# Feed-forward stages: the mean of squares taken by two float32r matmuls, one step later

## The chip, the cores and the metric

The kernel runs on one core of a Trainium2 chip. The core has five engines with queues of their own that meet only at semaphores: TensorE (PE, matmuls into PSUM; its weight loads are listed as PEld), VectorE (DVE), ScalarE (ACT), GpSimd (POOL) and SyncE (SP, which issues the DMAs). The metric is the device time of one execution in microseconds.

## The reference

A batch of 4 sequences of 1024 tokens with 128 channels goes through four blocks, each with a layer norm ahead of it and a residual around it: a first attention, a feed-forward stage, a causal attention, and the same feed-forward stage again. The change lies in the feed-forward stage, which runs twice. Each of its two layers is

```python
h = shift_token(x)                       # half of the channels comes from the token before
q, k, v = split(h @ wqkv, 3)             # 8 heads of 64
q, k = rotary_xpos(l2norm(q) * qs, l2norm(k) * ksc)
x = x + local_attention(q, k, v) @ wo    # windows of 64, the window before and its own
h = shift_token(x)
h = (h - h.mean(-1)) / sqrt(h.var(-1) + 1e-05) * lg + lb
a, g = split(h @ w1 + b1, 2)
x = x + (a * gelu(g)) @ w2 + b2
```

What changes is how `h.var` is computed: the mean over the channels of the squares of the centred `h`.

## The kernel before, in words

`ffn_stage` keeps channels on the partitions. Its work is cut into 64 tiles of 128 tokens (2 layers, 8 places, 4 sequences); four tiles of one place are a group `g`, and 512 columns of the second half of the layer (shift, norm, the two products `W1` and `W2`) are done for a whole group at a time. A loop over steps `i` is written out once for each engine, and at each step an engine does its parts of several tiles: the projection of tile `i+2` (`project_qk`, `project_v`), the transposes (`turn`) of tile `i+1`, the scores of tile `i`, the transposes of the probabilities (`turn_probs`) of tile `i-1` and the product with the values (`attend`) of tile `i-2`. Nothing but this order and the semaphores sets when something runs.

The parts of a group are hung on certain steps by `mlp_at`: "wo" at the second of four steps, "centre" and "mean" at the third, "w2" at the third or fourth, "gate01" at the fourth. At the third step PE multiplies `H2` by the centring matrix into the bank `m_ps[:, 0, :]` (L507), ACT squares that bank into `SQ2` (L657), and PE, as the last thing of the step, multiplies `SQ2` by the matrix `mean` (every entry 1/128) into `m_ps[:, 1, :]` (L561), in float32. At the next step ACT takes the logarithm and the exponential of that bank (L630, L632), which gives the reciprocal of the root, and DVE multiplies the centred bank by it into `HN` (L754).

The queues around this place, in order, are these. PE, third step: scores (L412, L421), centre (L507), `turn_probs` (L433), `turn` (L398), mean (L561); fourth step: `project_qk` (L379, which waits for DVE's copy `PT`, L786), `project_v` (L388, which waits for ACT's copy `QT`, L668), `attend` (L449), scores, `W2` (L500). ACT, third step: squares for the query norm (L638, which waits for DVE's rotary products L747), two copies (L649, L604), the square `SQ2`, eight exponentials of the scores (L594), the copy `QT`; fourth step: logarithm and exponential of the variance, then L638 again. POOL, every step: probabilities times reciprocal (L841), rotary sum (L847), a power (L853), which waits for DVE's clamped sums (L799).

Of the kernel before, what the change touches and what calls it, by code (L numbers as in the profile page):

```python
# [6 lines left out]
P = 128  # L7
NB, T = 4, 1024
NT = T // P
PAD = 4  # L10
EPS = 1e-5
F32 = mybir.dt.float32
# [138 lines left out]
def ffn_stage(nc, d, keep, stage):  # L151
# [5 lines left out]
    with nc.cleanup_on_exit(), ExitStack() as ctx:  # L157
# [33 lines left out]
        G = sb("G", [HC, NHC, NB * P])  # L191
        AG = sb("AG", [HC, NHC, NB * P])
        w0_ps, w1_ps, s_ps, m_ps = (ps(n, [P, 2, 512]) for n in ("w0", "w1", "s", "m"))
        nsq, nrs = [SQ2, H2], [RS, HN]

        s_set, s_qkv, s_qkv1, s_mlp_w, s_wo, s_w2, s_bias, s_folded, s_w1, s_rope, s_rope1, s_scaled, s_zero = (
# [24 lines left out]
        def real(x):  # L221
            return 0 <= x < TILES
# [40 lines left out]
        def norm_at(i):  # L263
            return i + EARLY if EARLY <= i + EARLY < NT and i >= 0 else None
# [68 lines left out]
        def _(pe):  # L333
            xt = X[:, :].rearrange("p (b t) -> p b t", b=NB)

            def norm_centre(t):
                if t >= EARLY:
                    pe.wait_ge(n_out, t)
                    pe.wait_ge(s_folded, 1)
                elif t >= 2:  # L340
                    pe.wait_ge(n_out, t - 1)
                pe.matmul(centre_bank(t), keep["centre"][:, :], xt[:, :, t * P:(t + 1) * P], start=True, stop=True)\
                  .then_inc(n_centred, 1)
# [109 lines left out]
            def hidden(g, half, j):  # L453
                pe.matmul(mlp_bank(g, half, j), W1[:, g // NT, half, j, :], HN[:, :], start=True, stop=True)\  # L454
                  .then_inc(gate_mm if half else value_mm, 1)

            norm_centre(0)
            norm_centre(1)
            norm_mean(0)
# [3 lines left out]
            for i in STEPS:  # L463
                g = mlp_at(i, "value1")
                if g is not None and g < LAST:
                    pe.wait_ge(gelu, 3 * g + 3)
                    hidden(g, 0, 1)
                if real(i + 2):
                    project_qk(i + 2)
                if norm_at(i) is not None:  # L470
                    norm_centre(norm_at(i))
                if real(i - 2) and values_first(i):
                    attend(i - 2)
                g = mlp_at(i, "gate2")
                if g is not None and g < LAST:
                    pe.wait_ge(gelu, 3 * g + 1)
                    hidden(g, 1, 2)
                if real(i + 2):
                    project_v(i + 2)
                g = mlp_at(i, "value0")  # L480
                if g is not None and g < LAST:
                    pe.wait_ge(hid, 3 * g + 1)
                    hidden(g, 0, 0)
                if real(i - 2) and not values_first(i):
                    attend(i - 2)
                if real(i):
                    score(i)
                if i == -1:
                    fold_bias()
                if norm_at(i) is not None:  # L490
                    norm_mean(norm_at(i))
                g = mlp_at(i, "w2")
                if g is not None:
                    pe.wait_ge(hid, 3 * g + 3)
                    if g + 1 < LAST:
                        pe.wait_ge(lnvar, g + 2)
                    if g == 0:
                        pe.wait_ge(s_w2, 16)
                    for j in range(NHC):
                        last = pe.matmul(m_ps[:, 1, :], W2[:, g // NT, j, :], AG[:, j, :], start=(j == 0),  # L500
                                         stop=(j == NHC - 1))
                    last.then_inc(w2_mm, 1)
                g = mlp_at(i, "centre")
                if g is not None:
                    pe.wait_ge(u, g + 1)
                    pe.wait_ge(s_h2[g % 2], 32 * (g // 2 + 1))
                    pe.matmul(m_ps[:, 0, :], keep["centre"][:, :], H2[:, :], start=True, stop=True).then_inc(centre_mm, 1)  # L507
                g = mlp_at(i, "value2")
                if g is not None and g < LAST:
                    pe.wait_ge(gelu, 3 * g + 2)  # L510
                    hidden(g, 0, 2)
                g = mlp_at(i, "gate01")
                if g is not None:
                    pe.wait_ge(hn, g + 1)
                    if g % NT == 0:
                        pe.wait_ge(s_w1, g // NT + 1)
                    if g < LAST:
                        hidden(g, 1, 0)
                if real(i - 1):
                    turn_probs(i - 1)  # L520
                if g is not None:
                    if g == LAST:
                        pe.wait_ge(pt, TILES)
                        pe.wait_ge(ot, TILES)
                        pe.wait_ge(kt, TILES)
                        pe.wait_ge(qt, TILES)
                        pe.wait_ge(probs, 2 * TILES)
                    elif g >= 1:
                        pe.wait_ge(ynext, g)
                    if g == LAST:  # L530
                        hidden(g, 1, 0)
                    hidden(g, 1, 1)
                    if g == LAST:
                        hidden(g, 1, 2)
                        hidden(g, 0, 2)
                        hidden(g, 0, 1)
                        hidden(g, 0, 0)
                if real(i + 1):
                    turn(i + 1)
                g = mlp_at(i, "wo")  # L540
                if g is not None:
                    pe.wait_ge(ot, NB * (g + 1))
                    if g >= 1:
                        pe.wait_ge(hid, 3 * g - 1)
                    else:
                        pe.wait_ge(n_out, NT)
                        pe.wait_ge(s_wo, 16)
                    for p in range(NPAIR):
                        last = pe.matmul(m_ps[:, 0, :], Wo[:, g // NT, p, :], OT[:, g % 2, p, :, :], start=(p == 0),
                                         stop=(p == NPAIR - 1))  # L550
                    last.then_inc(wo_mm, 1)
                g = mlp_at(i, "mean")
                if g is not None:
                    pe.wait_ge(sq2, g + 1)
                    if g >= 1:
                        pe.wait_ge(hid, 3 * g)
                    else:
                        pe.wait_ge(n_ln, NT)
                    if g == LAST:
                        pe.wait_ge(ynext, g)  # L560
                    pe.matmul(m_ps[:, 1, :], keep["mean"][:, :], SQ2[:, :], start=True, stop=True).then_inc(mean_mm, 1)  # L561

        @block.scalar
        def _(act):
# [48 lines left out]
            for i in STEPS:  # L613
# [39 lines left out]
                if g is not None:  # L653
                    act.wait_ge(centre_mm, g + 1)
                    if g >= 1:
                        act.wait_ge(mean_mm, g)
                    act.activation(SQ2[:, :], m_ps[:, 0, :], ACT.Square).then_inc(sq2, 1)  # L657
                if norm_at(i) is not None:
                    norm_square(norm_at(i))
                if real(i):  # L660
# [154 lines left out]
        def _(pool):  # L815
            pool.memset(mhalf[:, :], -0.5).then_inc(s_zero, 1)
            pool.memset(KT[:, :, :, :, :, :], 0.0).then_inc(s_zero, 1)
            pool.memset(Voff[:, :, :], 0.0).then_inc(s_zero, 1)

            def scale_rope(l, tiles):  # L820
                n = tiles.stop - tiles.start
# [13 lines left out]
            for i in STEPS:  # L835
                if real(i - 1):
                    x = i - 1
                    pool.wait_ge(rden, x + 1)
                    probs_x = PB[:, x % 2, :, :, :].rearrange("p e q k -> p (e q) k")
                    by = RDEN[:, x % 2, :, :].rearrange("p e q -> p (e q)").unsqueeze(2).broadcast_to([P, NH, P])  # L840
                    pool.tensor_tensor(probs_x, probs_x, by, ALU.mult).then_inc(normed, 1)  # L841
                if real(i + 2):
                    x = i + 2
                    pool.wait_ge(roped, x + 1)
                    if x >= 2:
                        pool.wait_ge(turned, 2 * x - 2)
                    pool.tensor_tensor(QK[:, x % 2, :, :, :].rearrange("p c q k -> p (c q k)"),  # L847
                                       T1[:, :, :, :].rearrange("p c h k -> p (c h k)"),
                                       T2[:, :, :, :].rearrange("p c h k -> p (c h k)"), ALU.add).then_inc(rope_sum, 1)
                    pool.wait_ge(clamped, x + 1)  # L850
                    if x >= 2:
                        pool.wait_ge(scaled, x - 1)
                    pool.tensor_tensor(RN[:, x % 2, :], SS[:, x % 2, :], mhalf[:, :], ALU.pow).then_inc(rnorm, 1)  # L853
                if i == 2:
                    pool.wait_ge(s_rope1, 16)
                    scale_rope(1, slice(0, NT))
# [1469 lines left out]
```

## Time and profile before

| | |
|---|---|
| median of 3 runs | 2151.45 us (2147.72 to 2151.94) |
| the profiled execution's own time | 2163.37 us |
| its span, from first to last instruction | 2161.6 us |
| mean granted TensorE clock | 0.967 |
| busy share of the span: PE, DVE, ACT, POOL | 92%, 83%, 63%, 57% |
| PE busy in the group from 430.30 to 471.20 us | 40.85 of 40.90 us |

A row of the timeline has the start in us from the span's start, the duration in us, the engine, the line, the operation, what it writes and reads, the shape, how many instructions were merged, and in brackets the idle time of the engine before it with what ended it. A float32 matmul stands in two instructions. PE's instructions are pipelined: each is listed until its result has drained, so the next one starts before it ends, and the distance of two starts is what one costs on PE.

### The profile page before, as it was taken

How to read it: one execution, taken by the hardware profiler on the slowest of the kernel's cores; microseconds unless marked ns; L12 is line 12 of the kernel's file. 1: busy time of each engine (PE TensorE's matmuls, PEld its weight loads, DVE VectorE, ACT ScalarE, POOL GpSimd, SP SyncE). 2: the span in 40 equal slices, each digit the busy share in tenths (PEclk: the TensorE clock that was granted, in tenths of full speed). 3: DMA queues.
4: the chain of work that ended last, by engine and by line, in shares of the span. 5: the costliest groups of instructions: out<-in, count | busy, mean ns of one | idle time of the engine just before them, and what ended most of it. 6: DMA issues, size and time to landing. Idle time of an engine off the chain costs nothing. (4 is left out here: it accounts for less than half of the span.)

```text
span 2161.6 us, 45550 instructions
## 1 busy us (share of the span) xinstructions
PE 1997.2 (92%) x16998; PEld 1096.8 (51%) x16998; DVE 1793.7 (83%) x2383; ACT 1366.5 (63%) x3435; POOL 1234.0 (57%) x599
## 2 busy tenths in 40 slices
PE   5686899999999999799999999967999999999997
PEld 2233555555555555345544444424555565555553
DVE  6986799999999996447888888537999999999993
ACT  8454566666666666325777777746667667666663
POOL 0116778778877875424222222247887877777770
PEclk9799999999999999969999999989999999999999
DMA  2003111211111110231322222022111111211111
GB/s 64 0 1 113 49 36 36 50 36 36 45 40 36 42 34 21 69 122 29 113 55 50 56 48 54 19 81 66 45 41 36 41 41 34 45 41 35 38 34 44
DMA packets 85473, 101.38 MB, mean 47 GB/s; under 512 B 13504, under 2 KB 60552, under 8 KB 83208
## 3 DMA queue, kind: packets, MB, share of 16 engines
q1 hardware_dynamic: 82824, 96.77, 17.8%
q8 instruction: 138, 2.26, 0.4%
q10 hardware_dynamic: 2432, 1.70, 0.3%
q14 instruction: 79, 0.65, 0.1%
HBM read 33.94 MB, written 10.49 MB: 21 GB/s over the span
## 5 line engine op out<-in xcount | busy, mean ns | idle before, releaser
L853 POOL TENSOR_TENSOR ffn_RN<-ffn_SS,ffn_mhalf 128x16 f32<-128x16 f32 x128 | 372.5, 2910 | 267.8 <-DVE ffn_SS L799 267.4
L2000 DVE TENSOR_REDUCE attn_b_NX<-attn_b_s 128x1 f32<-128x512 f32 (+3 forms) x608 | 365.1, 656 | 80.8 <-PE attn_b_s L1701 78.8
L847 POOL TENSOR_TENSOR ffn_QK<-ffn_T 128x1024 f32<-128x1024 f32 x128 | 420.4, 3284 | 20.1 <-DVE ffn_T L747 19.9
L594 ACT ACTIVATE ffn_PB<-ffn_s,ffn_NM 128x128 f32<-128x128 f32 x1024 | 360.3, 386 | 101.4 <-DVE ffn_NM L769 101.1
L1918 ACT ACTIVATE attn_b_PT<-attn_b_s 128x1024 f32<-128x1024 f32 (+1 forms) x320 | 284.0, 939 | 123.8 <-PE attn_b_s L1735 123.4
L638 ACT ACTIVATE ffn_SQ<-ffn_w 128x1024 f32<-128x1024 f32 x128 | 131.1, 1024 | 308.1 <-DVE ffn_T L747 307.7
L841 POOL TENSOR_TENSOR ffn_PB<-ffn_PB,ffn_RDEN 128x1024 f32<-128x1024 f32 x128 | 243.6, 1903 | 26.7 <-DVE ffn_RDEN L732 26.7
L379 PE MATMUL ffn_w<-ffn_Wqkv,ffn_H 128*128 128x512 f32 x512 | 245.4, 602 | 11.7 <-ACT ffn_SQ L638 4.7
L763 DVE TENSOR_TENSOR ffn_QK<-ffn_QK,ffn_RN 128x1024 f32<-128x1024 f32 x128 | 249.7, 1951 | 1.4 <-POOL ffn_RN L853 0.3
L594 ACT ACTIVATION_READ_ACCUMULATOR ffn_PB<-ffn_s,ffn_NM 128x1 f32 x1024 | 231.3, 226 | 0.0
L1701 PE MATMUL attn_b_s<-attn_b_KS,attn_b_QS 62*128 62x512 f32 (+3 forms) x768 | 228.2, 411 | 0.2
L786 DVE COPY ffn_PT<-ffn_w 128x1024 f32<-128x1024 f32 x128 | 156.2, 1220 | 74.3 <-PE ffn_w L433 74.3
L454 PE MATMUL ffn_m<-ffn_HN,ffn_W 128*114 128x512 f32 x360 | 189.3, 608 | 2.0 <-ACT ffn_G L622 2.0
L1735 PE MATMUL attn_b_s<-attn_b_QS,attn_b_KS 64*128 64x512 f32 (+3 forms) x768 | 171.9, 388 | 4.7 <-DMA attn_b_QS<-attn_b_MT 3.0
L744 DVE TENSOR_TENSOR ffn_T<-ffn_w,ffn_rope 128x1024 f32<-128x1024 f32 x128 | 154.3, 1205 | 19.2 <-PE ffn_w L379 19.1
L1754 PE MATMUL attn_b_o<-attn_b_PT,attn_b_VQ 128*32 128x512 f32 (+3 forms) x1536 | 165.3, 503 | 0.2
L747 DVE TENSOR_TENSOR ffn_T<-ffn_w,ffn_rope 128x512 f32<-128x512 f32 x256 | 163.6, 681 | 0.0
L449 PEld LDWEIGHTS ffn_w<-ffn_PT,ffn_Voff 128*64 128x64 f32 x2048 | 106.8, 137 | 108.4 <-issue 101.0
L769 DVE TENSOR_REDUCE ffn_NM<-ffn_s 128x8 f32<-128x1024 f32 x128 | 155.3, 1213 | 1.4 <-PE ffn_s L421 1.4
L379 PEld LDWEIGHTS ffn_w<-ffn_Wqkv,ffn_H 128*128 128x128 f32 x512 | 95.0, 193 | 121.1 <-issue 82.2
L796 DVE TENSOR_REDUCE ffn_SS<-ffn_SQ 128x16 f32<-128x1024 f32 x128 | 154.6, 1208 | 2.2 <-ACT ffn_SQ L638 2.2
L433 PEld LDWEIGHTS ffn_w<-ident,ffn_PB 128*128 128x128 f32 x1024 | 117.1, 143 | 76.4 <-issue 58.4
(250 smaller groups left out, 3791.4 us busy)
## 6 DMA issues: line engine op xcount, KB each, us to landing
ffn_Voff<-ffn_Vcur SPq DMA_DIRECT2D x248, 128.0 KB, 2.3
ffn_H<-ffn_Y SPq DMA_DIRECT2D x64, 128.0 KB, 2.5
ffn_H<-ffn_U SPq DMA_DIRECT2D x64, 128.0 KB, 2.5
attn_b_QS<-attn_b_qk_parts SPq DMA_DIRECT2D x64, 128.0 KB
attn_b_KS<-attn_b_qk_parts SPq DMA_DIRECT2D x64, 128.0 KB
attn_b_qk_parts<-attn_b_RP SPq DMA_DIRECT2D x6, 1024.0 KB, 7.5
ffn_rope<-in_ffn_rope_dram SPq DMA_DIRECT2D x4, 1024.0 KB, 7.8
attn_b_rope<-attn_b_OS SPq DMA_DIRECT2D x252, 16.0 KB
```

The costliest lines, as they stand in the source:

```text
L379: last = pe.matmul(w0_ps[:, c, :], H1[:, g % 2, b, :], Wqkv[:, l, c, :], start=True, stop=True)
L454: pe.matmul(mlp_bank(g, half, j), W1[:, g // NT, half, j, :], HN[:, :], start=True, stop=True)\
L594: last = act.activation(PB[:, x % 2, e, p, :], s_ps[:, e, p * P:(p + 1) * P], ACT.Exp, bias=NM[:, x % 2, e, p:p + 1], accum_out=DEN[:, x % ...
L763: dve.tensor_tensor(qk, qk, RN[:, x % 2, :].unsqueeze(2).broadcast_to([P, 2 * NH, DH]), ALU.mult)\
L841: pool.tensor_tensor(probs_x, probs_x, by, ALU.mult).then_inc(normed, 1)
L847: pool.tensor_tensor(QK[:, x % 2, :, :, :].rearrange("p c q k -> p (c q k)"), T1[:, :, :, :].rearrange("p c h k -> p (c h k)"), T2[:, :, : ...
L853: pool.tensor_tensor(RN[:, x % 2, :], SS[:, x % 2, :], mhalf[:, :], ALU.pow).then_inc(rnorm, 1)
L1701: last = pe.matmul(bank[:, q * width:(q + 1) * width], QS[rows, m % RING, pr, i * P:(i + 1) * P], KS[rows, m % RING, pr, c * 512:c * 512 + ...
L1735: last = pe.matmul(bank[par][:, q * w:(q + 1) * w], KS[rows, n % RING, first + q, j * P:(j + 1) * P], QS[rows, n % RING, first + q, lo:hi] ...
L1754: last = pe.matmul(o_ps[VCOLS * g:VCOLS * (g + 1), lo - half * 512:512], VQ[:, n % 2, g, j, :], PT[:, (n * NPIECE + s) % PRING, g, 0:hi - ...
L1918: act.activation(out, bank, ACT.Exp).then_inc(probs, 1)
L2000: dve.tensor_reduce(at, bank, AX_X, ALU.max, negate=True).then_inc(s1_read, 1)
```

## The change

The float32 matmul of `SQ2` by `mean` at the end of the third step goes. [...] POOL makes `meanr` once at the start of a stage.

```diff
+        SQH, SQL = (sb(name, [P, NB * P], F32R) for name in ("SQH", "SQL"))
+        meanr = sb("meanr", [P, P], F32R)
...
+            def mean_square(g):
+                if g == 0:
+                    pe.wait_ge(s_meanr, 1)
+                    pe.wait_ge(n_ln, NT)
+                else:
+                    pe.wait_ge(hid, 3 * g)
+                if g == LAST:
+                    pe.wait_ge(ynext, g)
+                pe.wait_ge(sq_hi, g + 1)
+                pe.matmul(m_ps[:, 1, :], meanr[:, :], SQH[:, :], start=True, stop=False)
+                pe.wait_ge(sq_lo, g + 1)
+                pe.matmul(m_ps[:, 1, :], meanr[:, :], SQL[:, :], start=False, stop=True).then_inc(mean_mm, 1)
...
                 if real(i + 2):
                     project_qk(i + 2)
+                g = mlp_at(i - 1, "mean")
+                if g is not None:
+                    mean_square(g)
...
-                g = mlp_at(i, "mean")
-                if g is not None:
-                    pe.wait_ge(sq2, g + 1)
-                    if g >= 1:
-                        pe.wait_ge(hid, 3 * g)
-                    else:
-                        pe.wait_ge(n_ln, NT)
-                    if g == LAST:
-                        pe.wait_ge(ynext, g)
-                    pe.matmul(m_ps[:, 1, :], keep["mean"][:, :], SQ2[:, :], start=True, stop=True).then_inc(mean_mm, 1)
...
                     act.activation(SQ2[:, :], m_ps[:, 0, :], ACT.Square).then_inc(sq2, 1)
+                    act.wait_ge(sq2, g + 1)
+                    act.activation(SQH[:, :], SQ2[:, :], ACT.Copy).then_inc(sq_hi, 1)
...
+            pool.tensor_copy(meanr[:, :], keep["mean"][:, :]).then_inc(s_meanr, 1)
...
+                g = mlp_at(i, "centre")
+                if g is not None:
+                    pool.wait_ge(sq_hi, g + 1)
+                    pool.tensor_tensor(SQL[:, :], SQ2[:, :], SQH[:, :].bitcast(F32), ALU.subtract).then_inc(sq_lo, 1)
+                if real(i + 2):
+                    x = i + 2
                     pool.wait_ge(clamped, x + 1)
```

The first place is PE's queue at the seam of the third and fourth step of a group, before the change; `ffn_SQ` stands for `SQ2`, `ffn_H` in the centre row for `H2`.

```order
L421 MATMUL ffn_s<-ffn_KT,ffn_QT 64x128 x16
L507 MATMUL ffn_m<-ffn_H,centre 128x512
L433 MATMUL ffn_w<-ident,ffn_PB 128x128 x8
L398 MATMUL ffn_w<-ident,ffn_QK 128x128 x8
L561 MATMUL ffn_m<-ffn_SQ,mean 128x512
L379 MATMUL ffn_w<-ffn_Wqkv,ffn_H 128x512 x2
L388 MATMUL ffn_w<-ffn_Wqkv,ffn_H 128x512
```

And the same place after the change, where the lines after the new code have moved by a few.

```order
L424 MATMUL ffn_s<-ffn_KT,ffn_QT 64x128 x16
L526 MATMUL ffn_m<-ffn_H,centre 128x512
L436 MATMUL ffn_w<-ident,ffn_PB 128x128 x8
L401 MATMUL ffn_w<-ident,ffn_QK 128x128 x8
L382 MATMUL ffn_w<-ffn_Wqkv,ffn_H 128x512 x2
L469 MATMUL ffn_m<-ffn_SQH,ffn_meanr 128x512
L471 MATMUL ffn_m<-ffn_SQL,ffn_meanr 128x512
L391 MATMUL ffn_w<-ffn_Wqkv,ffn_H 128x512
```

The mean has left the place between the transposes (L398, now L401) and `project_qk`, and its two successors stand between `project_qk` and `project_v`.

The second place is ACT's queue at the same step, after the change; before it, the row of `SQH` is absent and the others stand in the same order.

```order
L647 ACTIVATE ffn_SQ<-ffn_w 128x1024
L658 ACTIVATE ffn_Vcur<-ffn_w 128x512
L613 ACTIVATE ffn_OT<-ffn_w 128x4x128
L666 ACTIVATE ffn_SQ<-ffn_m 128x512
L668 ACTIVATE ffn_SQH<-ffn_SQ 128x512
L603 ACTIVATE ffn_PB,ffn_DEN<-ffn_s,ffn_NM 128x128 x8
L679 ACTIVATE ffn_QT<-ffn_w 128x512
L639 ACTIVATE ffn_RS<-ffn_m,eps 128x512
```

The new copy stands ahead of the eight exponentials and of `QT` (L679, before L668).

The third is POOL's queue at that step and the next, after the change.

```order
L853 TENSOR_TENSOR ffn_PB<-ffn_PB,ffn_RDEN 128x1024
L859 TENSOR_TENSOR ffn_QK<-ffn_T 128x1024
L865 TENSOR_TENSOR ffn_SQL<-ffn_SQ,ffn_SQH 128x512
L871 TENSOR_TENSOR ffn_RN<-ffn_SS,ffn_mhalf 128x16
L853 TENSOR_TENSOR ffn_PB<-ffn_PB,ffn_RDEN 128x1024
```

The subtraction stands between the rotary sum and the power. The queues of DVE and SP hold the same instructions in the same order as before.

## Rows read from the trace of the kernel before

**Rows 1.** The page, engines: busy us, share of the span, instructions.

```profile
PE 1997.2 (92%) x16998; PEld 1096.8 (51%) x16998; DVE 1793.7 (83%) x2383; ACT 1366.5 (63%) x3435; POOL 1234.0 (57%) x599
```

**Rows 2.** Busy time of each engine in one group of four steps.

```profile
430.30:471.20 40.90, 40.85 (x392) 24.13 (x391) 38.36 (x48) 27.62 (x89) 32.23 (x13) 1.00 0.17 40
```

**Rows 3.** Timeline of PE and its weight loads, seam of third and fourth step.

```profile
471.79 1.04 PE L398 MATMUL ffn_w<-ident,ffn_QK 128*128 128x128 f32 x8
...
472.67 1.02 PE L561 MATMUL ffn_m<-ffn_SQ,mean 128*128 128x512 f32 x2
...
473.27 0.45 PEld L379 LDWEIGHTS ffn_w<-ffn_Wqkv,ffn_H 128*128 128x128 f32 x2 [0.41 <-DVE ffn_PT L786]
...
473.53 1.88 PE L379 MATMUL ffn_w<-ffn_Wqkv,ffn_H 128*128 128x512 f32 x4
...
475.18 0.30 PEld L388 LDWEIGHTS ffn_w<-ffn_Wqkv,ffn_H 128*128 128x128 f32 x2 [0.60 <-ACT ffn_QT L668]
475.24 1.06 PE L388 MATMUL ffn_w<-ffn_Wqkv,ffn_H 128*128 128x512 f32 x2
...
478.53 2.84 PE L500 MATMUL ffn_m<-ffn_AG,ffn_W 114*128 114x512 f32 x6
```

**Rows 4.** Timeline of ACT, the same third step and the start of the fourth.

```profile
469.36 1.03 ACT L638 ACTIVATE ffn_SQ<-ffn_w 128x1024 f32<-128x1024 f32 x1 [4.24 <-DVE ffn_T L747]
...
471.24 0.62 ACT L657 ACTIVATE ffn_SQ<-ffn_m 128x512 f32<-128x512 f32 x1
...
471.71 0.40 ACT L594 ACTIVATE ffn_PB<-ffn_s,ffn_NM 128x128 f32<-128x128 f32 x1
...
474.45 0.68 ACT L668 ACTIVATE ffn_QT<-ffn_w 128x512 f32<-128x512 f32 x1
...
474.93 0.78 ACT L630 ACTIVATE ffn_RS<-ffn_m,eps 128x512 f32<-128x512 f32 x1
...
475.73 0.63 ACT L632 ACTIVATE ffn_RS<-ffn_RS 128x512 f32<-128x512 f32 x1
```

**Rows 5.** Timeline of DVE and POOL, from the third step to the fourth.

```profile
465.19 0.69 DVE L712 TENSOR_TENSOR ffn_U<-ffn_m,ffn_Y 128x512 f32<-128x512 f32 x1 [0.43 <-PE ffn_m L549]
...
469.25 1.22 DVE L763 TENSOR_TENSOR ffn_QK<-ffn_QK,ffn_RN 128x1024 f32<-128x1024 f32 x1
...
469.41 3.27 POOL L847 TENSOR_TENSOR ffn_QK<-ffn_T 128x1024 f32<-128x1024 f32 x1 [0.39 <-DVE ffn_T L747]
...
471.99 1.23 DVE L786 COPY ffn_PT<-ffn_w 128x1024 f32<-128x1024 f32 x1 [0.40 <-PE ffn_w L433]
...
473.13 1.21 DVE L796 TENSOR_REDUCE ffn_SS<-ffn_SQ 128x16 f32<-128x1024 f32 x1
...
474.63 2.91 POOL L853 TENSOR_TENSOR ffn_RN<-ffn_SS,ffn_mhalf 128x16 f32<-128x16 f32 x1 [1.95 <-DVE ffn_SS L799]
...
475.07 0.19 DVE L732 RECIPROCAL ffn_RDEN<-ffn_DEN 128x8 f32<-128x8 f32 x1
475.44 1.23 DVE L744 TENSOR_TENSOR ffn_T<-ffn_w,ffn_rope 128x1024 f32<-128x1024 f32 x1 [0.19 <-PE ffn_w L379]
...
477.51 1.90 POOL L841 TENSOR_TENSOR ffn_PB<-ffn_PB,ffn_RDEN 128x1024 f32<-128x1024 f32 x1
...
478.38 2.11 DVE L763 TENSOR_TENSOR ffn_QK<-ffn_QK,ffn_RN 128x1024 f32<-128x1024 f32 x1
```

**Rows 6.** Timeline of PE in the causal attention, whose operands are float32r tiles.

```profile
1205.28 0.40 PE L1701 MATMUL attn_b_s<-attn_b_KS,attn_b_QS 62*128 62x512 f32 x2
1205.50 0.41 PE L1735 MATMUL attn_b_s<-attn_b_QS,attn_b_KS 64*128 64x512 f32 x2
```

**Rows 7.** Groups by line: a POOL subtraction into float32r; busy us, mean ns.

```profile
L2082 POOL TENSOR_TENSOR attn_b_RP<-attn_b_TA,attn_b_RP 128x1024 fp32r<-128x1024 f32 x4 | 9.4, 2363 | 6.4 <-ACT attn_b_RP L1843 6.4
```

**Rows 8.** Timeline at the end of the first feed-forward stage, its last group.

```profile
869.88 0.60 ACT L657 ACTIVATE ffn_SQ<-ffn_m 128x512 f32<-128x512 f32 x1 [9.04 <-PE ffn_m L507]
870.53 1.12 PE L561 MATMUL ffn_m<-ffn_SQ,mean 128*128 128x512 f32 x2 [0.69 <-ACT ffn_SQ L657]
871.70 0.69 ACT L630 ACTIVATE ffn_RS<-ffn_m,eps 128x512 f32<-128x512 f32 x1 [1.22 <-PE ffn_m L561]
```

More of the change, by code:

```diff
@@ L193, in ffn_stage @@
         w0_ps, w1_ps, s_ps, m_ps = (ps(n, [P, 2, 512]) for n in ("w0", "w1", "s", "m"))
+        SQH, SQL = (sb(name, [P, NB * P], F32R) for name in ("SQH", "SQL"))
+        meanr = sb("meanr", [P, P], F32R)
+        s_meanr, sq_hi, sq_lo = sem("meanr"), sem("sq_hi"), sem("sq_lo")
         nsq, nrs = [SQ2, H2], [RS, HN]
```

## The prediction

> **What bounds the kernel now.** I read the page first, then the busy time of one group of four steps, then the timeline of the seam where the change lies. The page gives PE 92% of the span [rows 1], and within a group PE is listed busy for 40.85 of 40.90 us at full granted clock (1.00), while DVE has 38.36, POOL 32.23 and ACT 27.62 [rows 2]. So in the two feed-forward stages the order of PE's queue sets the pace, and another engine matters where it makes PE wait. That listing counts a matmul until it has drained, so short holes don't show in it; they show as starts further apart than the stream needs. A float32 instruction with 512 columns takes 0.43 us of stream: the four of `project_qk` start at 473.53 and what follows starts at 475.24, 1.71 us later [rows 3].
>
> At the seam two other engines are only just in time. `project_qk` needs DVE's copy `PT`, which runs from 471.99 and ends at 473.22 [rows 5]; its weights load at 473.27 with that copy named as the releaser, during the mean matmul, which streams from 472.67 to 473.53 [rows 3]. So the old mean filled a time in which PE had nothing else that it could do. Then `project_v` needs ACT's copy `QT`, which ends at 475.13 (474.45 + 0.68) [rows 4]; its weights load at 475.18, released by `QT`, and PE is free at 475.24 [rows 3]. Slack: none. I read these times for all groups: 28 of the 32 (14 in each stage) show this pattern; the last two groups of a stage differ, since no projection follows them.
>
> ACT at this place is one chain without a hole: it waits for DVE until 469.36, and from there to the end of `QT` each instruction starts before the one ahead has ended [rows 4]. The root of that chain is PE's product with `Wo`, for which DVE's `U` waits at 465.19 [rows 5]. So PE (`Wo`), DVE, ACT and PE (`project_v`) form a loop that goes round once in a group, and whatever lengthens ACT's part delays `project_v` by the same amount.
>
> **The change part by part.**
>
> *The mean leaves its old place.* That takes 0.86 us of stream (472.67 to 473.53) from PE. `project_qk` can't use it: its weights still load at 473.27, since `PT` is no earlier. Weights loaded while PE stands idle put off the first columns by about 0.1 us (475.18, then 475.71 for the second instruction of `project_v`, which is 0.10 more than one stream; the 475.71 is 475.24 + 1.06 less the 0.59 that a single instruction is listed, which is 1.88 less three times 0.43). So `project_qk` starts at 473.38 instead of 473.53 and ends at 475.09 instead of 475.24: 0.15 us of the 0.86 is gained, the rest becomes a hole.
>
> *The two new matmuls.* No row shows a float32r matmul with 128 rows. The nearest rows are those of the causal attention, whose tiles are float32r with 64 rows: one instruction for each product instead of two, and the next pair starts 0.22 us after the one before [rows 6]. Two of them cost 0.43 us, to 475.52. The lower bound is nothing (a price below that has no reason), the upper the float32 price of 0.85 each. I take 0.43, since the rows are of the same type and column count. At this price PE is ready for `project_v` at 475.52, which is 0.28 later than before, though half of the stream time was saved. In float32 it would be 475.09 + 1.71 = 476.80.
>
> *The copy `SQH` on ACT.* It stands between the square and the exponentials, and waits for the end of the square. The pair of logarithm and exponential shows the price of such a wait on the instruction just before: 474.93 + 0.78 = 475.71, and the next starts at 475.73 and takes 0.63 with SBUF on both sides [rows 4]. Now the square starts at 471.24 and the first exponential at 471.71, 0.15 before the square ends. With the copy: square to 471.86, copy from 471.88 to 472.51, first exponential 0.15 before that at 472.36. All that follows on ACT in this step is 0.65 us later; `QT` ends at 475.78. The bounds are 0.48 (no wait between the two, the mere distance of square and exponential) and 0.9; nothing lets it be hidden, since ACT has no idle time from 469.36 on.
>
> *What `QT` makes late.* The weights of `project_v` load at 475.83 instead of 475.18. PE, ready at 475.52, waits, and the rest of the group moves by 0.65 us: behind `project_v` in the queue stand the products with the values, the scores and `W2`, which is what starts at 478.53 [rows 3], and they all stream on. The next place where PE waits for others comes a step later and hangs on events after this one, so nothing is caught up there.
>
> *The exponentials also feed DVE.* The reciprocal at 475.07 needs their sums, which then are complete at 475.30; the rotary product after it, which now starts at 475.44 on PE's word, starts at about 475.47 [rows 5]. Nothing is lost there. The logarithm needs the mean matmul (475.52 and its drain, about 475.75) and follows `QT` at 475.8 anyway; DVE uses its result only after its three rotary products, for which it needs until about 478 (475.47 + 1.23 and as much again).
>
> *The subtraction on POOL.* The same subtraction of the same type stands in the causal attention, 2363 ns for 1024 columns [rows 7], so 1.18 us for 512; POOL's rotary sum of 1024 takes 3.27 beside DVE's work [rows 5], which would be 1.64. POOL is free at 472.68 (469.41 + 3.27) and `SQH` ready at 472.51, so `SQL` runs from 472.72 to between 473.9 and 474.4. The power at 474.63 waits for DVE until then [rows 5]: the subtraction lies in POOL's idle 1.95 us, and PE asks for it at 475.3. Cost: nothing. If it took 2.4 us, the power would slip by half a microsecond, and the work on POOL that follows it has more room than that before PE wants it.
>
> A row bears on whether POOL here slows DVE: the product of `QK` and `RN` takes 1.22 us when it starts before POOL's sum, and 2.11 when it starts at 478.38 inside POOL's product of 477.51 to 479.41 [rows 5]. The Trainium skill, "SBUF — State Buffer", section "Who interferes with whom", says that a VectorE instruction meets GpSimd only if both of its inputs lie in SBUF or it is in a two-port mode, and that a reduction never does on this chip. By that rule the reduction at 473.13 stays at 1.21 us under the subtraction and the third rival below falls; without it, it would be a likelier one. The rule agrees with the two rows, but no row has a POOL instruction beside this reduction.
>
> *The ends of the stages.* In the last group nothing else runs, so the chain is serial. Before: square to 870.48, mean from 870.53, logarithm at 871.70 [rows 8]. After: copy to 871.13, subtraction from 871.21 to 872.39, second matmul 0.11 + 0.21 + 0.21 until the logarithm (871.70 - 870.53 less the stream of 0.85 and 0.11 for the weights leaves 0.21), so 872.97: 1.27 us later. The group before it gets ACT's 0.65. That is 1.92 a stage, 3.8 for both. `meanr` is made while POOL waits for a table's DMA: nothing.
>
> *The sum.* 28 x 0.65 = 18.2, plus 3.8: 22.0 us. The profiled execution took 2163.4 us, so it would take 2185.4; the median of the timed runs is 11.9 us lower, and with the same difference the median comes to 2173.4, **2173 us** in round numbers.
>
> **The rivals.**
>
> *ACT isn't the one that decides (2162 us).* The timed runs are 11.9 us faster than the profiled one, up to 0.37 us a group; if that lies in ACT's chain, `QT` comes early enough, and only the hole before `project_qk` is left: 0.24 to 0.28 us a group, 28 x 0.24 + 3.8 = 10.5. For it speaks that difference; against it the unbroken chain of rows 4.
>
> *PE alone sets the pace, and the kernel gets faster (2143 us).* If `PT` and `QT` both came 0.6 us earlier against PE than the profile shows, `project_qk` would follow the transposes at once and PE would save 0.43 us a group: -12 + 3.8 = -8. It decides from the point at which the weights of `project_qk` load before 472.67. Against it: the load at 473.27 names `PT`, whose own wait names PE's transposes, so this chain is tied to PE and can't shift against it by much.
>
> *POOL holds DVE (2182 us).* If DVE's reduction at 473.13 were held until the subtraction ends, up to 1.2 us, DVE's chain of that step would come 1.2 later, the gelu of the fourth step after it, and the group would lose about 0.95 instead of 0.65: 28 x 0.95 + 3.8 = 30.4.
>
> *float32r is no cheaper (2199 us).* With 0.85 for each matmul `project_v` starts at 476.80, 1.52 later: 42.6, and with the ends some 48.
>
> **How the numbers follow.** Chances: the forecast 0.66, ACT not deciding 0.18, POOL holding DVE 0.08, float32r no cheaper 0.03, PE alone 0.05. What a measurement can tell from no change is about 0.2%, 4 us. Faster takes 0.04 of the last, and same takes the remaining 0.01 and 0.04 of a case in which timed runs have nearly the slack to hide it; slower is 0.91. The range, 2159 to 2184, holds the forecast with its bounds for the copy (28 x 0.48 and 28 x 0.9, with the 3.8, give 2169 and 2180), ACT not deciding and POOL holding DVE, with about 2 us either way for the clock at the ends of the stages, where PE idles and is granted half in some stretches.
>
> **What would show it.** In the profile after: the weights of `project_v` at the fourth step load about 0.65 us later after the square than the present 3.94, released by `QT`; the weights of `project_qk` still name `PT`; a hole before each. The two new matmuls are one instruction each, 0.2 us apart. POOL's power still waits for DVE's sums. A group of 40.9 us takes 41.5. If groups are shorter than now, or the load of `project_v` is released by PE's own queue, the loop through ACT was not what binds, and the forecast is wrong.

## The result, and the profile after

The changed kernel takes 2173.35 us (median of four runs, 2166.44 to 2178.53), the kernel before 2149.59 beside it (2146.86 to 2151.94): a ratio of 1.0108, 95% interval 1.0071 to 1.0146, so 15 to 31 us more. The forecast was 2173 in a range of 2159 to 2184. The profiled execution took 2178.2 us with a span of 2176.5.

First the page's row of engines after (columns as in [rows 1]), then the busy time from one square to the next (columns as in [rows 2]), in a group of the kernel before and in one of the changed kernel.

```profile
PE 1995.9 (92%) x16998; PEld 1097.7 (50%) x16998; DVE 1796.7 (83%) x2383; ACT 1393.3 (64%) x3467; POOL 1275.1 (59%) x633
```

```profile
430.30:471.24 40.94, 40.90 (x392) 24.17 (x391) 38.40 (x48) 27.66 (x90) 32.27 (x13) 1.00 0.17 40
```

```profile
516.56:558.17 41.61, 40.93 (x392) 24.11 (x390) 38.27 (x48) 28.44 (x90) 33.49 (x14) 1.00 0.17 39
```

PE is listed busy for 1.3 us less in the whole, and the clock of the group is the full one, yet the group takes 41.61 us where it took 40.94 from square to square. The row of engines can't show the loss: in the stretch between the two stages alone PE is listed busy for 5.5 us less (604.03 and 598.55, in the last section), at another share of half clock. The lengthening is the same through a stage: the second to the ninth distance of two squares are near 40.94 before and near 41.61 after, the next four near 41.54 and 42.22. The first distance of each stage stays what it was (40.52 and 40.39 before, 40.41 and 40.41 after), and the last two vary between executions by up to a microsecond.

What happens stands in the timeline of the seam of third and fourth step (start us, duration us, engine, line, operation; in brackets the idle time before and its releaser). `ffn_SQH` is ACT's float32r copy of the squares, `ffn_SQL` what POOL's subtraction of that copy leaves, and `ffn_meanr` the float32r copy of the matrix `mean`:

```profile
558.17 0.62 ACT L666 ACTIVATE ffn_SQ<-ffn_m 128x512 f32<-128x512 f32 x1
...
558.82 0.63 ACT L668 ACTIVATE ffn_SQH<-ffn_SQ 128x512 fp32r<-128x512 f32 x1
558.93 1.23 DVE L797 COPY ffn_PT<-ffn_w 128x1024 f32<-128x1024 f32 x1 [0.40 <-PE ffn_w L436]
559.36 0.35 ACT L603 ACTIVATE ffn_PB<-ffn_s,ffn_NM 128x128 f32<-128x128 f32 x1
...
559.58 1.27 POOL L865 TENSOR_TENSOR ffn_SQL<-ffn_SQ,ffn_SQH 128x512 fp32r<-128x512 f32 x1
...
560.07 1.21 DVE L807 TENSOR_REDUCE ffn_SS<-ffn_SQ 128x16 f32<-128x1024 f32 x1
...
560.21 0.30 PEld L382 LDWEIGHTS ffn_w<-ffn_Wqkv,ffn_H 128*128 128x128 f32 x2 [0.68 <-DVE ffn_PT L797]
560.21 1.98 PE L382 MATMUL ffn_w<-ffn_Wqkv,ffn_H 128*128 128x512 f32 x4 [0.45 <-DVE ffn_PT L797]
...
561.57 2.91 POOL L871 TENSOR_TENSOR ffn_RN<-ffn_SS,ffn_mhalf 128x16 f32<-128x16 f32 x1 [0.71 <-DVE ffn_SS L810]
...
561.63 0.80 PE L469 MATMUL ffn_m<-ffn_SQH,ffn_meanr 128*128 128x512 f32 x1
...
562.10 0.64 ACT L679 ACTIVATE ffn_QT<-ffn_w 128x512 f32<-128x512 f32 x1
562.26 0.40 PE L471 MATMUL ffn_m<-ffn_SQL,ffn_meanr 128*128 128x512 f32 x1
562.28 0.20 DVE L743 RECIPROCAL ffn_RDEN<-ffn_DEN 128x8 f32<-128x8 f32 x1 [0.20 <-ACT ffn_PB L603]
...
562.79 0.30 PEld L391 LDWEIGHTS ffn_w<-ffn_Wqkv,ffn_H 128*128 128x128 f32 x2 [0.57 <-ACT ffn_QT L679]
562.79 1.13 PE L391 MATMUL ffn_w<-ffn_Wqkv,ffn_H 128*128 128x512 f32 x2
```

Count everything from the start of the square. `project_qk` loads its weights at 2.04 as before (2.03, [rows 3]), still released by `PT`, and PE idles 0.45 us ahead of it. PE is ready for `project_v` at 4.32: the columns of `project_qk` begin 0.10 after the load and stream for 1.71, to 562.02, and two instructions of 0.23 follow, the second at 562.26. (The first is listed from 561.63, while `project_qk` still streams, so here the distance of the two listed starts isn't the price.) But `QT` ends at 4.57 (before 3.89), and the weights of `project_v` load at 4.62 (before 3.94), 0.30 us after PE is ready, with `QT` as the releaser. In all 28 groups that have this seam the load stands 4.60 to 4.62 after the square, before 3.92 to 3.94. The first exponential stands at 1.19 after the square (before 0.47, [rows 4]).

The rows that answer to [rows 6, 7] are groups by line (busy us, mean ns of one):

```profile
L865 POOL TENSOR_TENSOR ffn_SQL<-ffn_SQ,ffn_SQH 128x512 fp32r<-128x512 f32 x32 | 40.6, 1269 | 35.1 <-ACT ffn_SQH L668 35.0
...
L471 PE MATMUL ffn_m<-ffn_SQL,ffn_meanr 128*128 128x512 f32 x32 | 13.0, 406 | 2.3 <-POOL ffn_SQL L865 2.3
```

One instruction a product, 32 for 32 groups, and 0.23 us of stream each (from the end of `project_qk` at 562.02 to 562.26; in the split on POOL below from 476.43 to 476.66): float32r has the price that the attention's tiles showed. The end of the first stage answers to [rows 8]; the logarithm starts 3.19 us after the square, where it started 1.82 after it:

```profile
881.08 0.60 ACT L666 ACTIVATE ffn_SQ<-ffn_m 128x512 f32<-128x512 f32 x1 [9.03 <-PE ffn_m L526]
881.71 0.63 ACT L668 ACTIVATE ffn_SQH<-ffn_SQ 128x512 fp32r<-128x512 f32 x1
882.41 1.27 POOL L865 TENSOR_TENSOR ffn_SQL<-ffn_SQ,ffn_SQH 128x512 fp32r<-128x512 f32 x1 [14.77 <-ACT ffn_SQH L668]
...
883.74 0.49 PE L471 MATMUL ffn_m<-ffn_SQL,ffn_meanr 128*128 128x512 f32 x1 [0.79 <-POOL ffn_SQL L865]
884.27 0.69 ACT L639 ACTIVATE ffn_RS<-ffn_m,eps 128x512 f32<-128x512 f32 x1 [1.94 <-PE ffn_m L471]
```

### The profile page after: what moved, and what is told of

Read it like the earlier page. It is cut to its first block and busy times, and to the rows that moved or that the text cites. A ratio compares the mean times of both kernels' runs of the same rounds, so it can differ in the third digit from the quotient of the medians.

```text
span 2176.5 us, 45616 instructions
## 1 busy us (share of the span) xinstructions
PE 1995.9 (92%) x16998; PEld 1097.7 (50%) x16998; DVE 1796.7 (83%) x2383; ACT 1393.3 (64%) x3467; POOL 1275.1 (59%) x633
## 5 line engine op out<-in xcount | busy, mean ns | idle before, releaser
L871 POOL TENSOR_TENSOR ffn_RN<-ffn_SS,ffn_mhalf 128x16 f32<-128x16 f32 x128 | 372.8, 2913 | 250.3 <-DVE ffn_SS L810 249.9
L603 ACT ACTIVATION_READ_ACCUMULATOR ffn_PB<-ffn_s,ffn_NM 128x1 f32 x1024 | 222.1, 217 | 0.0
```

What stands on the lines that cost most here:

```text
L603: last = act.activation(PB[:, x % 2, e, p, :], s_ps[:, e, p * P:(p + 1) * P], ACT.Exp, bias=NM[:, x % 2, e, p:p + 1], accum_out=DEN[:, x % ...
```

## The experiments

The theory: `project_v` starts at the later of two arrivals, PE's own queue and `QT` through ACT, and the group follows that start one for one. The rivals were that PE's work alone counts, that POOL holds DVE, and that the new place, not the copy, costs the time. All were timed in five rounds against the kernel before. "Group" is the distance of neighbouring squares in a typical group of that run's profile (before 40.94).

| kernel | us | ratio, 95% interval | group |
|---|---|---|---|
| copy alone | 2164.68 | 1.0085, 1.0056 to 1.0113 | 41.61 |
| new place alone | 2167.19 | 1.0091, 1.0059 to 1.0124 | 41.61 |
| split on POOL | 2163.12 | 1.0055, 1.0029 to 1.0081 | 41.21 |
| one float32r matmul, old place | 2150.28 | 1.0002, 0.9977 to 1.0028 | 40.95 |
| after, values ahead of `project_v` | 2166.74 | 1.0077, 1.0049 to 1.0104 | 41.41 |
| before, values ahead of `project_v` | 2162.23 | 1.0042, 1.0017 to 1.0067 | 41.16 |
| split at the old place | 2170.54 | 1.0105, 1.0072 to 1.0138 | 41.68 |

The kernel before took 2145.60 beside the first four and 2150.81 beside the last three. The ratio isn't the quotient of the two medians: single executions of the kernel before lie between 2137.73 and 2159.85 us, and ratio and quotient differ by up to 0.3%.

**The copy alone.** The kernel before, with ACT's copy, which nobody reads.

```
...
                     act.activation(SQ2[:, :], m_ps[:, 0, :], ACT.Square).then_inc(sq2, 1)
+                    act.wait_ge(sq2, g + 1)
+                    act.activation(SQH[:, :], SQ2[:, :], ACT.Copy).then_inc(sq_hi, 1)
```

> The kernel before with one thing added: ScalarE copies the squares into a float32r tile right after squaring; nobody reads the copy, and the float32 mean stays at its old place. Theory (the loop through ScalarE: its exponentials and QT come later, and project_v waits for QT): project_v's weights load 0.65 us later after the square (3.94 becomes about 4.6), a group takes 40.94 + 0.66 = 41.6 us, in all 28 x 0.66 and 0.65 at the end of each stage = about +20 us. Rival (PE's hole before project_qk is what costs): the hole is still filled by the mean, so no change.

Timeline of its seam, whose square starts at 473.62:

```profile
475.90 1.88 PE L381 MATMUL ffn_w<-ffn_Wqkv,ffn_H 128*128 128x512 f32 x4
...
477.55 0.63 ACT L672 ACTIVATE ffn_QT<-ffn_w 128x512 f32<-128x512 f32 x1
...
478.23 0.30 PEld L390 LDWEIGHTS ffn_w<-ffn_Wqkv,ffn_H 128*128 128x128 f32 x2 [1.28 <-ACT ffn_QT L672]
```

PE's side is untouched (`project_qk` at 2.28 after the square, before 2.29), and `project_v` still loads at 4.61. The copy on ACT is enough by itself for the whole loss of a group.

**The new place alone.** The kernel before, with its float32 mean moved behind `project_qk`.

```
...
                     project_qk(i + 2)
+                g = mlp_at(i - 1, "mean")
+                if g is not None:
...
+                    pe.matmul(m_ps[:, 1, :], keep["mean"][:, :], SQ2[:, :], start=True, stop=True).then_inc(mean_mm, 1)
...
```

> The kernel before with one thing moved: the float32 mean stands between project_qk and project_v of the next step; no split, no copy, no subtraction. Theory (the old mean filled a hole that PT leaves, so 0.71 of its 0.86 us become visible): project_qk starts 0.15 earlier, project_v can start at 475.09 + 0.86 = 475.95 in the clock of the first trace instead of 475.28, a group takes 0.66 longer, about +18 us in all. Rival (only ScalarE's copy counts, moving work within PE's queue costs nothing): no change.

Its seam, square at 475.24:

```profile
477.27 1.98 PE L379 MATMUL ffn_w<-ffn_Wqkv,ffn_H 128*128 128x512 f32 x4 [0.44 <-DVE ffn_PT L786]
...
478.45 0.68 ACT L668 ACTIVATE ffn_QT<-ffn_w 128x512 f32<-128x512 f32 x1
...
479.09 1.02 PE L479 MATMUL ffn_m<-ffn_SQ,mean 128*128 128x512 f32 x2
479.52 0.19 PEld L388 LDWEIGHTS ffn_w<-ffn_Wqkv,ffn_H 128*128 128x128 f32 x1 [0.24 <-issue]
479.95 1.02 PE L388 MATMUL ffn_w<-ffn_Wqkv,ffn_H 128*128 128x512 f32 x2
```

Here the releaser is another: the weights of `project_v` are loaded ahead ("issue", no `QT`), for `QT` ended at 479.13, and PE's queue is what comes last, at 4.71. So the move of a float32 mean costs as much as the copy. In the changed kernel, where the shorter matmuls make PE ready at 4.32, the two delays don't add: the group is 41.61 there too.

**The split on POOL.** The changed kernel, with `SQH` copied by POOL.

```
-                    act.wait_ge(sq2, g + 1)
-                    act.activation(SQH[:, :], SQ2[:, :], ACT.Copy).then_inc(sq_hi, 1)
...
+                    pool.wait_ge(sq2, g + 1)
+                    pool.tensor_copy(SQH[:, :], SQ2[:, :]).then_inc(sq_hi, 1)
```

> The changed kernel with the copy SQH made by GpSimd, ahead of its subtraction, instead of ScalarE. Theory (two causes, of which the later one decides): with ScalarE's chain as before, what is left is the hole before project_qk and the two float32r matmuls, 0.24 to 0.4 us a group, 7 to 11 us, and about 1.4 us at the end of each stage, so +10 to +14 us; the weights of project_v are no longer released by QT. Rival (ScalarE's copy is the whole cost): +3 us from the ends alone. Second rival (GpSimd's longer work holds VectorE or comes late for PE): +20 us or more.

Its seam, square at 472.34:

```profile
473.73 0.61 POOL L863 CAST ffn_SQH<-ffn_SQ 128x512 fp32r<-128x512 f32 x1
...
474.42 1.28 POOL L865 TENSOR_TENSOR ffn_SQL<-ffn_SQ,ffn_SQH 128x512 fp32r<-128x512 f32 x1
...
475.56 0.68 ACT L677 ACTIVATE ffn_QT<-ffn_w 128x512 f32<-128x512 f32 x1
...
476.43 0.40 PE L471 MATMUL ffn_m<-ffn_SQL,ffn_meanr 128*128 128x512 f32 x1
...
476.66 1.02 PE L391 MATMUL ffn_w<-ffn_Wqkv,ffn_H 128*128 128x512 f32 x2
```

With `QT` back at 3.90, `project_v` starts at 4.32, straight behind the two matmuls: what is left, 0.27 us a group, is the hole ahead of `project_qk` and the two streams.

**One float32r matmul at the old place.** The kernel before; ACT writes the squares as float32r, and one matmul takes them. The squares' low bits are left out.

```
...
-                    act.activation(SQ2[:, :], m_ps[:, 0, :], ACT.Square).then_inc(sq2, 1)
+                    act.activation(SQH[:, :], m_ps[:, 0, :], ACT.Square).then_inc(sq2, 1)
...
-                    pe.matmul(m_ps[:, 1, :], keep["mean"][:, :], SQ2[:, :], start=True, stop=True).then_inc(mean_mm, 1)
+                    pe.matmul(m_ps[:, 1, :], meanr[:, :], SQH[:, :], start=True, stop=True).then_inc(mean_mm, 1)
```

> The kernel before with its mean at the old place, but as one float32r matmul: ScalarE writes the squares as float32r, so the low bits of the squares are left out of the mean. It takes 0.64 us of stream from PE in each group and adds nothing to any engine. Theory (the hole before project_qk and the wait for QT stay): project_qk gains at most 0.15 us, project_v nothing, so 0 to -0.1 us a group, 0 to -4 us in all. Rival (PE's stream sets the pace): 28 x 0.64 and the ends, -19 us.

Its seam, square at 470.01:

```profile
471.35 0.47 PE L565 MATMUL ffn_m<-ffn_SQH,ffn_meanr 128*128 128x512 f32 x1
...
472.04 1.99 PE L382 MATMUL ffn_w<-ffn_Wqkv,ffn_H 128*128 128x512 f32 x4 [0.21 <-DVE ffn_PT L790]
...
473.96 0.30 PEld L391 LDWEIGHTS ffn_w<-ffn_Wqkv,ffn_H 128*128 128x128 f32 x2 [0.76 <-ACT ffn_QT L672]
```

Three quarters of the mean's stream are gone (0.86 us becomes 0.23), no instruction is added in a group, and the time is the same within 0.3%. `project_qk` waits for `PT` all the same, and `project_v` for `QT` (load at 3.95). PE alone doesn't set this pace.

**The values ahead of `project_v`.** In the fourth step too, PE multiplies with the values first; once in the changed kernel, once in the kernel before.

```
-            return i % NB == 0 or not real(i + 2)
+            return i % NB in (0, 3) or not real(i + 2)
```

> The changed kernel with project_v and attend of the group's fourth step exchanged (on PE and, with them, their two copies on ScalarE); the copy SQH stays on ScalarE and QT stays 0.65 us late. Theory (the whole of that lateness is paid by PE standing before project_v): attend needs nothing of QT, so PE works on it while QT arrives, and only the hole before project_qk and the two matmuls remain: a group of 41.2 to 41.35 us instead of 41.61, +11 to +14 us against the kernel before. Rival (ScalarE's lateness costs through VectorE or a later copy, not through this wait): a group stays at 41.6, +20 us.

> The kernel before with the same exchange of project_v and attend, nothing else. Theory: PE reaches this place at 475.24 in the clock of the first trace and the wait for QT costs it 0.04 us, so there is nothing to win: a group of 40.9 to 40.95 us, 0 to -1 us. If the exchange itself had an effect of its own (the copies on ScalarE, the transfer of the values), a group would differ by 0.1 us or more, and the run above would have to be read against it.

The control missed: the exchange isn't free, it costs the kernel before 0.22 us a group. The start of `project_qk` and two weight loads in the seam of that control (square at 470.61), and after them the start of `W2`:

```profile
472.90 1.88 PE L379 MATMUL ffn_w<-ffn_Wqkv,ffn_H 128*128 128x512 f32 x4
...
474.74 0.23 PEld L449 LDWEIGHTS ffn_w<-ffn_PT,ffn_Voff 128*64 128x64 f32 x4 [0.80 <-issue]
...
475.85 0.30 PEld L388 LDWEIGHTS ffn_w<-ffn_Wqkv,ffn_H 128*128 128x128 f32 x2
```

```profile
478.12 0.70 PE L500 MATMUL ffn_m<-ffn_AG,ffn_W 114*128 114x512 f32 x1
```

The products with 64 columns of weights now stand between two products with 128. The stream of `project_qk` ends at 474.61 (472.90 + 1.71) and the weights of the values load after it, at 474.74; those of `project_v` load at 475.85, behind the products with the values. That this change of width is what costs the 0.22 us is a reading of these rows; no run tests it alone. `W2` starts 7.51 after the square, in the kernel before 7.29 [rows 3]. Against this control the changed kernel with the same exchange loses 41.41 - 41.16 = 0.25 us; the 41.41 itself is above the 41.2 to 41.35 expected, by the price of the exchange. Its `QT` is as late as ever (4.57), but other work covers it, and the remainder is near that of the split on POOL (0.27). Read against the plain kernel before, it would have looked as though the exchange had won back only 0.20 of the 0.67.

**The split at the old place.** The changed kernel with its two matmuls where the mean stood.

```
-                g = mlp_at(i - 1, "mean")
-                if g is not None:
-                    mean_square(g)
...
+                g = mlp_at(i, "mean")
+                if g is not None:
+                    mean_square(g)
```

> The changed kernel with its two float32r matmuls at the old place, at the end of the third step, so the split alone without the move. With times counted from the start of the square as the changed kernel's trace shows them: the subtraction ends at 2.61, so the second matmul runs to 2.98 and project_qk starts there instead of at 2.14, ending at 4.69; QT is ready at 4.56 and its wait ends at 4.62. Theory (the later of PE and QT decides): project_v moves from 4.04 to 4.73 or 4.8, a group takes 41.6 to 41.75 us, within 0.15 us of the changed kernel, +20 to +24 us. Rival (the move to the later place was what kept the split from costing more, since PE stands still for the subtraction): a group of 42.2 us or more, +38 us.

Its seam, square at 473.69:

```profile
476.42 0.19 PEld L471 LDWEIGHTS ffn_m<-ffn_SQL,ffn_meanr 128*128 128x128 f32 x1 [1.15 <-POOL ffn_SQL L865]
...
476.77 1.88 PE L382 MATMUL ffn_w<-ffn_Wqkv,ffn_H 128*128 128x512 f32 x4
...
478.30 0.38 PEld L391 LDWEIGHTS ffn_w<-ffn_Wqkv,ffn_H 128*128 128x128 f32 x2 [0.48 <-ACT ffn_QT L679]
478.48 1.02 PE L391 MATMUL ffn_w<-ffn_Wqkv,ffn_H 128*128 128x512 f32 x2
```

Now PE waits for POOL ahead of `project_qk` and is ready at 4.79, just behind `QT`, whose weights were in place at 478.40. So the place one step later buys 0.07 us a group, no more, as long as the copy is on ACT.

**All seven on one line.** In the seams shown, for each kernel that keeps the order of `project_v` and the values, when PE was ready, when the first columns could follow `QT` (0.10 after the load of the weights; where `QT` releases no load, 0.15 after its end), and the group; all counted from the square.

| kernel | PE ready | `QT`'s way | group | group less the later |
|---|---|---|---|---|
| before | 4.00 | 4.04 | 40.94 | 36.90 |
| one float32r matmul | 3.84 | 4.05 | 40.95 | 36.90 |
| split on POOL | 4.32 | 4.05 | 41.21 | 36.89 |
| copy alone | 3.99 | 4.71 | 41.61 | 36.90 |
| new place alone | 4.71 | 4.04 | 41.61 | 36.90 |
| after | 4.32 | 4.72 | 41.61 | 36.89 |
| split, old place | 4.79 | 4.71 | 41.68 | 36.89 |

The rest of a group is 36.9 us in all of them. In these groups a group is that rest and the later arrival.

## Why the prediction was right

Its loop through ACT is what binds, and the prices at the seam came within 0.1 us. One step doesn't hold throughout: that nothing is caught up behind the seam.

- *The old mean filled a hole.* Shown: the weights of `project_qk` load where they did, and one float32r matmul in its place gains nothing. PE ready: 4.28 predicted, 4.32 measured.
- *Two float32r matmuls, 0.43.* Measured 0.23 each, so 0.46.
- *The copy, 0.65 on ACT's chain.* Measured 0.68 at `QT`, 0.67 in the group; "copy alone" shows that the copy does it.
- *The subtraction is hidden.* It took 1.27 us, not 1.18, and ended at 2.68 after the square, before PE asks at 4.1. POOL's power still waits for DVE (L871, released by `SS`). The reduction under the subtraction took 1.21 as before, and the copy alone, without any subtraction, loses the same 0.67 a group; so the rival in which POOL holds DVE falls. The Trainium skill, "SBUF — State Buffer", section "Who interferes with whom", says that on this chip a reduction never contends with GpSimd. This trace agrees: POOL's 559.58 to 560.85 overlaps DVE's 560.07 to 561.28.
- *Nothing is caught up behind the seam.* Wrong for the first group of each stage. There the load of `project_v` is as late as elsewhere (4.61), but one step later PE used to wait for `PT` and now doesn't; before and after, counted from the squares at 266.94 and 267.88, `project_qk` starts at 11.69 and 11.57:

```profile
278.63 1.98 PE L379 MATMUL ffn_w<-ffn_Wqkv,ffn_H 128*128 128x512 f32 x4 [0.53 <-DVE ffn_PT L786]
```

```profile
279.45 1.98 PE L382 MATMUL ffn_w<-ffn_Wqkv,ffn_H 128*128 128x512 f32 x4
```

- *Ends of the stages, 1.27.* Measured 1.37 (3.19 less 1.82); the subtraction's 1.27 instead of 1.18 is most of the difference.
- *The sum, 22.0.* With measured terms, for 26 groups instead of 28: 26 x 0.67 + 2 x (1.37 + 0.67) = 21.5. In the two profiles the stages grow, from first to last square, by 10.26 us (602.94 to 613.20) and 7.81 (604.42 to 612.23); with 1.37 at each end that is 20.8. The ratio gives 23.2 us, with 15 to 31 inside its interval. That the sum lies so close is in part luck: the two groups too many more than make up for terms taken a little small.
- *ACT isn't the one that decides.* The 11.9 us by which the profiled execution was slower than the timed ones, on which this rival rested, go with the clock: of the 26 executions of the kernel before beside the first four experiments the fastest (2137.73 us) had a mean granted clock of 0.978, the two slowest (2159.84 and 2159.85) 0.967 and 0.964, the profiled one 0.967. The copy alone shows that ACT does decide. The split on POOL shows this rival as a kernel of its own: 0.27 a group, where the prediction gave 0.24 to 0.28.

What it didn't say: that a float32 mean in the new place costs as much as the copy. Its own numbers held that (0.86 less 0.15 is 0.71 later; measured 4.71 against 4.00), but it weighed the mean in float32 only as a rival about float32r's price.

## What to carry to other kernels

Where an engine looks 100% busy, look for the two or three instructions whose weights load only on another engine's word. In this kernel work queued ahead of such loads was free as long as PE was through with it before the last word came (a mean of 0.86 us or of 0.23 us gave the same time); the same 0.86 us one load further on cost 0.67 a group, and a copy on the engine that gives the word cost as much though that engine's own share is 64%. Two such delays at one meeting point combine as a maximum, so taking away one of them may win back nothing; list both arrivals. Run the control for a rescheduling on the old kernel as well, since the exchange has its own price.

## What was not expected of the hardware

The profiled spans differ by 14.9 us (2161.6 and 2176.5), not by 23. The stretch between the stages, mostly the causal attention, is the reason: without it the spans differ by 21.8 us. Windows from the last square of the first stage to the first of the second, before and after (columns as in [rows 2]; the clock is the third number from the right):

```profile
869.88:1528.61 658.73, 604.03 (x4779) 296.13 (x4780) 478.15 (x780) 402.02 (x578) 226.88 (x214) 0.94 0.23 63
```

```profile
881.08:1532.88 651.80, 598.55 (x4779) 295.26 (x4780) 478.24 (x780) 402.66 (x580) 228.87 (x216) 0.95 0.23 64
```

The change touches this stretch only at its start, where it adds 1.37 us, and yet it is 6.9 us shorter: 68.3 us of it at a granted clock of 0.5 (1.2 GHz), against 78.5 before. Over the nine profiles the time at half clock in this stretch varies from 37.5 us (640.31 and 641.99 us long) to 78.5 (653.01 and 658.73). Two stretches with the same 78.5 differ by 5.7 us, so the half clock isn't all of it. Why PE is granted half there in one execution and not in the next stays open. For a change of 1% the distance of two squares, which mostly repeats within 0.1 us among like groups, is a better measure than the span of one profile.
